# Negated maxima carried to stacked rows by small transfers, picking products left out, and the score banks divided four to three

## The reference, cut to what matters

```
h = tok(x)                                             # grey value, Scharr filter, absolute values
h = h + attn(layernorm(h), Wq, bq, Wk, bk, Wv, bv, Wp)
h = h + ffn(layernorm(h), ...)                         # ffn has a norm and a residual of its own

# attn
q = (x @ Wq + bq) per head @ Wp;  k = (x @ Wk + bk) per head @ Wp;  v = x @ Wv + bv
scores = q . k / sqrt(16)                              # [batch, token, head, token]
out = softmax(scores) @ v
```

## Time and profile before

| what | value |
|---|---|
| median of three runs | 308.85 us |
| the profiled execution | 308.78 us, span 307.0 us |
| TensorE busy | 286.5 us (93%) |
| VectorE busy | 213.6 us (70%) |
| ScalarE busy | 161.4 us (53%) |
| GpSimd busy | 132.1 us (43%) |
| granted TensorE clock | 1.00 of full speed, mean over the span |

### The profile page before, as it was taken

How to read it: one execution, slowest core, us unless ns; L and a number is a source line. 1 busy time by engine, 2 the same in 40 slices (tenths; PEclk the granted TensorE clock), 3 DMA queues, 4 the chain that set the end, 5 groups by cost and what they waited for, 6 DMA issues and landing times.

```text
span 307.0 us, 6170 instructions
## 1 busy us (share of the span) xinstructions
PE 286.5 (93%) x2280; PEld 224.3 (73%) x2280; DVE 213.6 (70%) x423; ACT 161.4 (53%) x304; POOL 132.1 (43%) x250
## 2 busy tenths in 40 slices
PE   0499999999999999999999999898999999999996
PEld 0378878887677766666666666565898988989976
DVE  8978984785799988888889888634835734642332
ACT  1391453523333478768777876776344434434440
POOL 7605240330200018862859562066759489500000
DMA  6978019895398971678582000000000200200202
GB/s 211 324 191 270 2 69 288 181 217 206 108 281 252 326 270 55 183 185 270 162 174 76 4 3 2 0 2 2 0 1 2 69 2 0 68 2 0 70 0 68
DMA packets 26631, 35.30 MB, mean 115 GB/s; under 512 B 5082, under 2 KB 15594, under 8 KB 26602
## 3 DMA queue, kind: packets, MB, share of 16 engines
q1 hardware_dynamic: 26440, 34.77, 38.0%
q10 hardware_dynamic: 162, 0.15, 0.1%
HBM read 24.42 MB, written 10.49 MB: 114 GB/s over the span
## 4 chain that ended last, share of the span: by engine, by line
PE 81%; DVE 13%; ACT 3%; issue 2%; ACTq 0%; DVEq 0%
PE bank L1139 46%; PE bank L1257 9%; PE bank L1209 8%; PE bank L1232 4%; PE bank L1237 4%; DVE negmax L848 3%; PE bank L1275 3%; PE bank L1267 1%; DVE gray L725 1%; PE bank L1161 1%; PE bank L1283 1%; PE bank L1176 1%; DVE qk_l L838 1%; DVE gray L724 1%; DVE xn L813 1%
## 5 line engine op out<-in xcount | busy, mean ns | idle before, releaser
L848 DVE TENSOR_REDUCE negmax<-bank 128x2 f32<-128x512 f32 x128 | 82.0, 684 | 6.1 <-PE bank L1209 5.8
L1047 ACT ACTIVATE probs<-bank 128x512 f32<-128x512 f32 x128 | 66.1, 602 | 28.2 <-PE bank L1237 28.2
L902 DVE TENSOR_TENSOR y_l<-yf,y_h 128x512 fp32r<-128x512 f32 x32 | 23.7, 743 | 39.1 <-ACT yf L1073 39.0
L1070 ACT ACTIVATE y_h<-bank,b1col 128x512 fp32r<-128x512 f32 x32 | 22.1, 689 | 47.8 <-PE bank L1139 47.8
L1139 PE MATMUL bank<-w_h,y_h 128*128 128x256 f32 x128 | 36.9, 289 | 2.5 <-DVE y_l L902 2.1
L1139 PE MATMUL bank<-w_h,y_l 128*128 128x256 f32 x128 | 36.2, 282 | 0.0
L1139 PE MATMUL bank<-w_l,y_h 128*128 128x256 f32 x128 | 36.2, 282 | 0.0
L1257 PE MATMUL bank<-probs,vals 128*32 128x256 f32 x512 | 34.3, 385 | 0.0
L1209 PE MATMUL bank<-ks,qs 48*128 48x256 f32 x256 | 32.2, 329 | 1.3 <-DVE negmax L848 0.7
L1209 PEld LDWEIGHTS bank<-ks,qs 48*128 48x128 f32 x256 | 19.3, 184 | 15.7 <-DVE negmax L848 6.4
L1139 PEld LDWEIGHTS bank<-w_h,y_h 128*128 128x128 f32 x128 | 24.4, 190 | 4.6 <-DVE y_l L902 3.6
(11 more groups left out here) (147 smaller groups left out, 612.6 us busy)
## 6 DMA issues: line engine op xcount, KB each, us to landing
xr<-in_x SPq DMA_DIRECT2D x8, 768.0 KB, 9.0
qs<-qk_parts SPq DMA_DIRECT2D x48, 128.0 KB, 3.3
ks<-qk_parts SPq DMA_DIRECT2D x48, 128.0 KB, 3.4
qk_parts<-qk_h SPq DMA_DIRECT2D x16, 256.0 KB, 3.2
qk_parts<-qk_l SPq DMA_DIRECT2D x16, 256.0 KB, 3.5
wraw<-in_L_ffn_fc_q SPq DMA_DIRECT2D x4, 512.0 KB, 4.6
wscale<-in_L_ffn_fc_scales SPq DMA_DIRECT2D x4, 512.0 KB, 6.7
out<-osb SPq DMA_DIRECT2D x16, 128.0 KB, 1.8
```

Source lines behind the costliest of these rows:

```text
L848: eng.tensor_reduce(negmax[:, b % 2, u, v], entry_bank(key)[:, :].rearrange("p (t k) -> p t k", t=NT), AX.X, ALU.max, negate=True).then_in ...
L902: eng.tensor_tensor(y_l[:, p % 2, f], yf[:, n % 2], y_h[:, p % 2, f].bitcast(fp32), ALU.subtract).then_inc(s_y, 1)
L1047: eng.activation(probs[:, n % PBUF], p2[n % 4][:, :], ACT.Exp).then_inc(s_exp, 1)
L1070: eng.activation(y_h[:, p % 2, f], src, ACT.Silu, bias=b1col[:, f:f + 1])
```

## The change

What it does, part by part:

- `pick`, `picked` and the 128 picking matmuls go. `qs` gets two more rows per half (48 and 49, and 112 and 113) that hold the two parts of the negated maxima, and `ks` gets ones there; the four key matmuls contract 50 rows and start their banks themselves.
- The rows of ones are loaded once by four transfers from a cleared-to-one tile. `pass_neg`, new on SyncE, sends each half image's rows from `negrow` (now 16 rows) into `qs`, with two transfers of 8 KB, after ScalarE's copy. `scores_by_key` waits for them (`s_nld`) instead of for the copy.
- In SyncE's order `pass_neg(0, 0)` stands behind the second store of the last pair, `pass_neg(0, 1)` behind the fourth, and the others at the beginning of the step after the negation, ahead of that step's loads.
- The ring for scores by query has four banks (0 to 3) all through the loop; the scores by key have three (4 to 6), and slot s waits for the first exponential of slot s - 1.
- TensorE's and VectorE's order: keys of s first, then, for even s, the queries (the maxima) of s + 10 and s + 11 together.
- The first products of the feed-forward stage use the banks 2, 3, 1.

```diff
-    NCOL = HALF + SPLIT
+    KSTACK = SPLIT + 2
...
-    negrow = at("negrow", 18.75, [NCOL, 2, N], fp32r)
+    negrow = at("negrow", 18.75, [16, 2, N], fp32r)
...
-    negsplit = at("negsplit", 24.125, [P, NT, NCOL], fp32)
+    negsplit = at("negsplit", 24.125, [P, NT, 16], fp32)
+    ones = at("ones", 24.25, [2, P], fp32)
...
-        p2 = bank[3:7]
+        p2 = bank[4:7]
...
         for s in range(END):
-            if s + AHEAD < SLOTS:
-                head_entries(s + AHEAD)
+            if s % 2 == 0:
+                for k in (s + AHEAD, s + AHEAD + 1):
+                    if k < SLOTS:
+                        head_entries(k)
...
-                r = n % 4 if n < in_a else n % 3
+                r = n % 4
...
-        F1_BANKS = (2, 1, 3)
+        F1_BANKS = (2, 3, 1)
...
+            def pass_neg(b, half):
+
+                wait_drained(eng, ("neg", b, half))
+                if b >= 4:
+                    eng.wait_ge(s_p2, UNITS * (b - 4) + 4 * (half + 1))
+                cols = slice((b % 2) * N, (b % 2 + 1) * N)
+                for v in range(2):
+                    row = HALF * v + SPLIT
+                    eng.dma_start(qs[row:row + 2, (b // 2) % 2, half * 4:(half + 1) * 4, cols].bitcast(fp32),
+                                  negrow[8 * v:8 * v + 8, half, :].bitcast(fp32)).then_inc(s_nld[half], 16)
...
+            eng.wait_ge(s_zero, 3)
+            for r in range(2):
+                for v in range(2):
+                    row = HALF * v + SPLIT
+                    eng.dma_start(ks[row:row + 2, r].rearrange("p u (c n) -> p (u c) n", n=P).bitcast(fp32),
+                                  ones[:].unsqueeze(1).broadcast_to([2, UNITS * COLS // P, P])).then_inc(s_ones, 16)
             for b in range(4, B):
                 load_x(b)
...
             for i in range(4):
                 store_qk(3, i)
+                if i == 1:
+                    pass_neg(0, 0)
+            pass_neg(0, 1)
...
             for s in range(SLOTS):
+                if s >= 1 and neg_after(s - 1):
+                    pass_neg(*neg_after(s - 1))
                 for p in (2, 3):
...
-            link(eng.memset(negsplit[:], 0.0))
+            eng.memset(ones[:], 1.0).then_inc(s_zero, 1)
...
-            eng.wait_ge(s_ident, 1)
-            link(eng.tensor_reduce(picked[:], ident[:].rearrange("p (v c r u) -> p u v c r", v=2, c=8, r=2)[:, :, :, 0], AX.XY, ALU.add))
-            eng.tensor_copy(pick[:], picked[:]).then_inc(s_pick, 1)
             gray_add(0)
...
             def neg_rows(b, half):
                 key = ("neg", b, half)
                 wait_entry(eng, key)
                 if b >= 1:
-                    eng.wait_ge(s_p2, UNITS * (b - 1) + 4 * (half + 1))
-                eng.activation(negrow[:, half], entry_bank(key)[0:NCOL, 0:N], ACT.Copy).then_inc(s_neg, 1)
+                    eng.wait_ge(s_nld[half], 32 * b)
+                eng.activation(negrow[:, half], entry_bank(key)[0:16, 0:N], ACT.Copy).then_inc(s_neg, 1)
...
                 if s == 0:
-                    eng.wait_ge(s_pick, 1)
-
-                    wait_drained(eng, [key for key in entries[:in_a] if ebank[key] == 3][-1])
+                    eng.wait_ge(s_ones, 64)
                 if u % 4 == 0:
-                    wait_drained(eng, ("neg", b, u // 4))
+                    eng.wait_ge(s_nld[u // 4], 32 * (b + 1))
...
-                if n >= 4:
-                    eng.wait_ge(s_exp, n - 2)
-                for v in range(2):
-                    rows = slice(HALF * v, HALF * v + SPLIT)
-                    eng.matmul(p2[(n + v) % 4][:, :].rearrange("p (t n) -> p t n", t=NT), pick[rows, u % 4:u % 4 + 1].broadcast_to([SPLIT, P]),
-                               negrow[rows, u // 4].unsqueeze(1).broadcast_to([SPLIT, NT, N]), start=True, stop=False)
+                if n >= 2:
+                    eng.wait_ge(s_exp, n - 1)
                 for t in range(NT):
                     for v in range(2):
-                        rows = slice(HALF * v, HALF * v + SPLIT)
-                        ins = eng.matmul(p2[(n + v) % 4][:, t * N:(t + 1) * N], ks[rows, r, u, c + t * P:c + (t + 1) * P],
-                                         qs[rows, r, u, c:c + N], start=False, stop=t == NT - 1)
+                        rows = slice(HALF * v, HALF * v + KSTACK)
+                        ins = eng.matmul(p2[(n + v) % 3][:, t * N:(t + 1) * N], ks[rows, r, u, c + t * P:c + (t + 1) * P],
+                                         qs[rows, r, u, c:c + N], start=True, stop=True)
...
             for s in range(END):
-                if s % 2 == 0 and s + AHEAD < SLOTS:
-                    scores_by_query(s + AHEAD)
                 if s < SLOTS:
                     scores_by_key(s)
-                if s % 2 == 1 and s + AHEAD < SLOTS:
-                    scores_by_query(s + AHEAD)
+                if s % 2 == 0:
+                    for k in (s + AHEAD, s + AHEAD + 1):
+                        if k < SLOTS:
+                            scores_by_query(k)
```

More of the change, by code:

```diff
@@ L82, in vit_tower_kernel @@
     unused = at("unused", 18.375, [P, 1], fp32)
-    pick = at("pick", 18.5, [P, 4], fp32r)
-    picked = at("picked", 18.5625, [P, 4], fp32)
-    negrow = at("negrow", 18.75, [NCOL, 2, N], fp32r)
+    negrow = at("negrow", 18.75, [16, 2, N], fp32r)
     b2 = at("b2", 20.75, [P, E], fp32)
@@ L184, in vit_tower_kernel @@
         s_border = sem("gray_borders_zeroed")
-        s_pick = sem("pick_ready")
+        s_ones = sem("rows_of_ones_loaded")
+        s_nld = [sem("neg_rows_loaded0"), sem("neg_rows_loaded1")]
         s_band = sem("band_ready")
@@ L310, in vit_tower_kernel @@
                 head_entries(HEAD_AT[key])
-        in_a = len(entries)
         for s in range(END):
-            if s + AHEAD < SLOTS:
-                head_entries(s + AHEAD)
+            if s % 2 == 0:
+                for k in (s + AHEAD, s + AHEAD + 1):
+                    if k < SLOTS:
+                        head_entries(k)
             if neg_after(s):
@@ L335, in vit_tower_kernel @@
             held[r] = key
-        in_b = [[key for key in entries if ebank[key] == r and not (key[0] == "n3" and key[1] >= 1)][-1] for r in range(3)]
+        in_b = [[key for key in entries if ebank[key] == r and not (key[0] == "n3" and key[1] >= 1)][-1] for r in range(4)]
         def entry_bank(key):
@@ L550, in split_max @@
                 src = negmax[:, b % 2, half * 4:(half + 1) * 4].rearrange("p u v t -> p v t u")
-                hi, lo = ([negsplit[:, :, HALF * v + 4 * part:HALF * v + 4 * part + 4] for v in range(2)] for part in range(2))
+                hi, lo = ([negsplit[:, :, 8 * v + 4 * part:8 * v + 4 * part + 4] for v in range(2)] for part in range(2))
                 for v in range(2):
@@ L953, in _ @@
             for s in range(END):
-                if s + AHEAD < SLOTS:
-                    largest(s + AHEAD)
+                if s % 2 == 0:
+                    for k in (s + AHEAD, s + AHEAD + 1):
+                        if k < SLOTS:
+                            largest(k)
                 if s in (SLOTS - 1, SLOTS + 1):
@@ L1046, in exp_head @@
                     eng.wait_ge(s_av, (n - PBUF) // 4 + 1)
-                eng.activation(probs[:, n % PBUF], p2[n % 4][:, :], ACT.Exp).then_inc(s_exp, 1)
+                eng.activation(probs[:, n % PBUF], p2[n % 3][:, :], ACT.Exp).then_inc(s_exp, 1)
             def neg_rows(b, half):
@@ L1248, in attend @@
                     if G == 0:
-                        eng.wait_ge(s_zero, 4)
+                        eng.wait_ge(s_zero, 5)
                         wait_read(eng, last_turns[3])
@@ L1266, in neg @@
                 for t in range(NT):
-                    ins = eng.transpose(entry_bank(key)[0:NCOL, t * P:(t + 1) * P], negsplit[:, t], ident[:])
+                    ins = eng.transpose(entry_bank(key)[0:16, t * P:(t + 1) * P], negsplit[:, t], ident[:])
                 ins.then_inc(s_ent, 1)
@@ L1291, in fc1 @@
                         eng.wait_ge(s_w1r, 4)
-                    if n < 2:
+                    if n < 3:
                         wait_drained(eng, in_b[r])
-                    elif n == 2:
-                        eng.wait_ge(s_exp, 2 * SLOTS)
                     else:
```

2 lines of the change are left out of this document (1 added, 1 removed).

## The result

The changed kernel takes **327.01 us** (median of 4 runs, 325.58 to 327.85) against 308.87 for the kernel before (4 runs, 308.30 to 309.14) on the same chip: **1.0585 times as long, [1.0544, 1.0626]**. The sign was forecast; 18.1 us are far more than 4.6, and beyond the range.

A forecast was written before the change was run, and what follows sets the result against it. TensorE was taken as the bound (busy 13.17 of 13.26 us a batch), VectorE 1.8 us behind. Terms -0.3 - 2.3 + 3.7 + 3.0 - 0.2 + 0.7 = +4.6 on 308.8 gave 313.4 us, range 305 to 318.

The forecast's parts named there:

- The sign: Whole kernel: slower, chance 0.72 in all, against 0.10 for the same and 0.18 for faster.
- GpSimd: Weight loads move by 1.8 us, but GpSimd has the whole loop to split them: no cost.
- the start: Beginning of the kernel: without the reduction and cast for `pick`, the first VectorE chain is shorter, -0.3 us.
- the pair: Plain pair of slots in the attention loop: 2.57 us, set by VectorE's maxima, instead of 2.79.
- covered by 0.06: Three key banks: exponential ready 1.06 after a slot starts; with queries between, the next starts at 1.12 anyway, no wait.
- the 15 pairs: Pairs with queries outside the stretches that SyncE sets: together -2.3 us, from -6.2 to 0.
- 0.25, 0.26, 0.12 and +0.05 a pair: Per pair: plain -0.25, with a negation -0.26, with an output -0.12, with both +0.05 us.
- the clock as a rival of 0.17: Idle TensorE before slots 0 and 24 lowers the clock, 2.4 us each: 315.8 or 318.2 us; chance 0.17.
- slots 12 to 24: Slot 24 waits for a small transfer behind loads and 1 MB of weights: +3.0 us, from +1.4.
- slots 28 to 40: Slot 40's small transfer, with no weights ahead, lands about in time: -0.2 us, to -1.3.
- the first slot: Slot 0 waits for its transfer behind a store, landing 3.4 after the second issue: +3.7 us (2.1 to 4.5).
- the tail: Last five pairs, no queries between key sets: key bank waits +0.25 each, less 0.3, in all +0.7 us (0 to 1.5).

The follow-up runs named there:

- experiment 4: Kernel before with the small transfers instead of the picks, its banks and order kept: 320.36 us, 1.0362.
- experiment 5: Changed kernel with the second layer's four weight loads one step later, behind the transfer that slot 24 waits for: 322.67 us, 1.0458.
- experiment 2: Changed kernel with the clock held up by unread transposes on TensorE ahead of slots 0, 24 and 40: 317.4 us, 1.0293.
- experiment 8: Changed kernel, image 0's transfers earlier, two loads a slot, weight loads one a slot: 308.16 us; banks and order of before 307.13; fourth key bank 303.83.
- experiment 6: Changed kernel, image 0's transfers earlier, two loads a step, second layer's weights one step later: 321.36 us; old banks 322.3; fourth key bank 316.8.
- experiment 7: Changed kernel with small transfers issued by GpSimd, SyncE's order as before: 318.56 us; old banks and order 315.62; fourth key bank 314.77.
- experiment 1: Changed kernel with small transfers issued by ScalarE right after its copy, not by SyncE: 324.65 us, 1.0506.

## Why the prediction was right about the sign and wrong about the size

**Right: where it would be lost.** Slot 0 and slot 24 wait for `pass_neg` behind SyncE's queue, the key pairs at the end wait for their bank, and VectorE runs dry behind the late slots. GpSimd and the start are as forecast (the filter's first matmul 0.16 us earlier, 0.3 forecast).

**Right in size, not in the engine: the pair.** A plain pair of the kernel after, from key set to key set, and VectorE's maxima right behind it:

```profile
118.18 0.51 PE L1252 MATMUL bank<-qs,ks 50*128 50x256 f32 x4
118.53 0.69 PE L1230 MATMUL bank<-ks,qs 48*128 48x256 f32 x8
119.38 0.50 PE L1252 MATMUL bank<-qs,ks 50*128 50x256 f32 x4 [0.16 <-ACT probs L1068]
119.81 1.07 PE L1272 MATMUL bank<-probs,vals 128*32 128x256 f32 x16
120.81 0.50 PE L1252 MATMUL bank<-qs,ks 50*128 50x256 f32 x4
...
121.65 2.48 DVE L867 TENSOR_REDUCE negmax<-bank 128x2 f32<-128x512 f32 x4 [0.20 <-PE bank L1230]
```

2.63 us against 2.57 forecast, and the batch 12.52 against 12.70. But the forecast had VectorE back to back at 2.57, and VectorE takes 2.48 here, and before the maxima of the next pair (last row) it waits 0.20 for TensorE's queries. What sets the pair is TensorE's own chain: 1.20 from key set to key set, with the wait of 0.16 for the exponential (third row) that I had taken as covered by 0.06, then 0.43 and 1.00. That this comes to nearly 2.57 is luck. With the clock held up the stretches of the 15 pairs (0 to 12, 24 to 28, 40 to 54) give -1.2 - 0.5 - 1.7 = -3.4, where -2.3 was forecast. (The forecast's 0.25, 0.26, 0.12 and +0.05 a pair don't follow from its rows, which give 2.79 - 2.57 = 0.22, 0.21, 0.04 and -0.07; by the same counts these, too, add up to -2.3.)

**Wrong: the clock as a rival of 0.17.** The step that failed is the one that named idle times of 4.5 and 3.9 us before slots 0 and 24, said that the loop never does that, and still took a clock of 1.00 in the forecast. The idle times came (4.3 and 6.8), a third came (4.4), and the clock fell each time. The rival's price was 2.4 each; the runs give 2.4, 3.5 and 2.5, 8.4 in all. What was missed is that the drop is a consequence of the lateness and no accident beside it, so that nearly all cases with late slots needed it: in experiments 4 and 5 the clock fell behind all three waits again. The Trainium skill ("TensorE: Matmul & The Clock Gate", "HAM oscillation") describes transfers' waits followed by bursts at the low clock, and the trace agrees; the rival that named it should have had most of the chance.

**Wrong: slots 12 to 24, +5.6 for +3.0.** The landing behind 1 MB was right: 3.3 us from the end of the issue (146.44 to 149.78) where 3.4 was taken. The issues before it were priced 2.7 us too low: a start 0.17 later, three small pairs at 1.26 to 1.36 instead of 0.9 (+1.28), twelve loads at 8.31 and 8.39 instead of 7.56, each with one long issue (+1.58), gaps between the groups (+0.42), weights at 1.08 instead of 1.82 (-0.74). An 8 KB issue takes 0.62 us in the median of 32, as a 128 KB load does; I had taken a store's 0.45.

**Wrong: slots 28 to 40, not -0.2.** The same cost of issues, and a slip: at 3.4 from the start of the second issue, as for slot 0, the forecast's own landing would be Y + 20.75, not Y + 20.3, and the term +0.25. In experiment 2 the issue of `pass_neg(5, 0)` ended 19.7 behind slot 28, not 17.8, which with 1.7 for landing would be +0.9. In the kernel after the two long loads put it at 22.0, and so slot 40 at +3.3. Its wait of 4.4 us was not forecast, and it cost the third drop.

**Wrong: the first slot, in the other direction.** The pair was issued at 101.73 and slot 0 began at 104.49, not 105.9. The landing was the part that failed: from the start of the second issue the small transfers take 2.0 to 2.4 us wherever only loads of 128 KB and stores are in flight (slots 0, 20, 36, 40), so the 3.4 from the nearest loads was too much. The Trainium skill's 2 us fixed cost ("DMA: Bandwidth & Descriptors", "Anatomy of one DMA"), which it gives for transfers issued by GpSimd, was the better price also for SyncE's, and gave the measured +2.3.

**Wrong: the tail, +2.0 for +0.7.** TensorE's timeline of the kernel after, one of the last pairs, and of the kernel before, likewise:

```profile
207.03 0.50 PE L1252 MATMUL bank<-qs,ks 50*128 50x256 f32 x4
208.22 0.50 PE L1252 MATMUL bank<-qs,ks 50*128 50x256 f32 x4 [0.69 <-ACT probs L1068]
```

```profile
195.00 0.50 PE L1232 MATMUL bank<-negrow,pick 48*128 48x512 f32 x2
...
196.12 1.07 PE L1257 MATMUL bank<-probs,vals 128*32 128x256 f32 x16
```

Slot s + 1 starts 1.19 behind slot s, and `attend` then 0.43 later: 1.62 in place of the 1.12 (195.00 to 196.12) of the kernel before, +0.50 where +0.25 was forecast. The step that failed took 1.06 for the first part and 0.31 for the second. The first of the five pairs took 4.06 us against 4.02, since TensorE waited there for ScalarE's copy in both kernels (0.46 after, 0.87 before); four pairs at +0.50 are the +2.0. The fourth key bank, which takes these waits away alone, is worth 4.3, 4.6 and 3.8 us between the medians of three versions (experiments 8, 6, 7), and from slot 54 to the end 3.6 in each of the three pairs of traces. That is more than the +2.0, because without picks and without waits a pair's key sets mostly take 0.67 us up to `attend`, less than the 1.12 of the kernel before.

In sum, with the clock held up, the terms came to +1.7 - 3.4 + 5.6 + 2.3 + 2.0 = +8.2 where +4.6 was forecast; the clock added 8.4 and the 1.6 of experiment 2 the rest.

**Left open.** Whether the new bank division without the fourth key bank is better over the whole kernel than the old one: 308.16 against 307.13 overlap, and the clock of the first varies from run to run. What makes single loads hold SyncE for 2 us, why the first packet of a small transfer starts late behind bytes issued from another queue, and which waits the clock forgives were not tried further; the runs show only that it happens. No trace shows the kernel with every transfer in time and no drop; of experiment 8's runs those with a clock of 1.00 took 305.3 to 306.0 us, and with the fourth key bank 302.3.

## What to carry to other kernels

A transfer that stands between two instructions of a loop cost here what its queue and the bytes in flight made of it, and not what its own size suggests: before putting one there, write down the issue time of everything ahead of it on that queue, and look for large loads near it. If the bounding engine then waits longer than it ever does now, price the lower clock into the forecast itself. And products that look like overhead may fill time that a ring of banks leaves empty: change the ring and the products together, and give back banks to whoever needs them when a phase of the loop ends.

## What was unexpected of the hardware

- A transfer of 8 KB within SBUF holds SyncE for 0.62 us, ScalarE for 0.64 and GpSimd for 0.57: as long as the issue of 128 KB. From SyncE's queue it let its reader start 2.0 to 2.4 us after its issue began beside loads of 128 KB, 4.0 behind 1 MB and 6.2 behind 2 MB; from GpSimd's queue 7.1 behind 2 MB.
- The granted clock fell to the lower level not only after waits of 4 to 7 us, but also after one of 1.5 us (experiment 1) and of 2.0 and 1.26 (experiment 8), in a loop that is otherwise dense, and not after one of 1.75 (experiment 7). The three drops of the kernel after, of 7 to 14 us each, cost 2.4 to 3.5 us.
- Transposes that nobody reads (14, 50 and 30, in three waits) kept the clock at 1.00; 8.4 us of the 9.9 that the span lost lie in the stretches behind these waits.
